# Where the first part's last rows are stored, how many buffers hold a finished block, and how the last two quantised tiles are cut

## The reference, cut to what matters

```python
x = x + xattn(layernorm(x), ctx_512, Wq, Wkv, Wout)   # causal attention, 16 heads
x = x + attn(layernorm(x), w_gate, g_gate, w_down, g_down)
#   bitlinear twice: rmsnorm, rows rounded to 8 bits, weights to -1, 0, 1; 256 -> 2 x 1024 -> 256
x = x + ffn(layernorm(x), gate_w, w_gate, w_up, w_down)
#   16 experts of width 176, each token goes to its best 6, weighted by its softmax scores
return x
```

## Time and profile before

| | |
|---|---|
| three runs, median | 595.3 to 598.86 us, 598.38 us |
| profiled execution | 599.67 us, its span 597.9 us |
| busy, share of the span | PE 83%, DVE 71%, POOL 68%, ACT 59% |
| the barrier between the blocks | about 229 to 230 us |
| the second part's adds (POOL, L1436) | first at 393.6, last at 571.2 us |
| behind the last add | 571.2 to 597.9 us |

### The profile page before, as it was taken

How to read it: one execution, slowest core, us unless ns; L and a number is a source line. 1 busy time by engine, 2 the same in 40 slices (tenths; PEclk the granted TensorE clock), 3 DMA queues, 4 the chain that set the end, 5 groups by cost and what they waited for, 6 DMA issues and landing times.

```text
span 597.9 us, 13765 instructions
## 1 busy us (share of the span) xinstructions
PE 494.3 (83%) x3930; PEld 423.0 (71%) x3952; DVE 427.5 (71%) x1233; ACT 353.2 (59%) x765; POOL 408.5 (68%) x465
## 2 busy tenths in 40 slices
PE   5788999896888865693998999799999999999800
PEld 4567778674555543572998999689998999999800
DVE  5776778868998965797786767367667667668515
ACT  3586665555887973362675666356666666666500
POOL 5743957674886764476777776288887888888860
PEclk9999999979998986596998999799999999999955
DMA  9999994000000004397799775578887888888678
GB/s 253 332 327 328 327 328 159 1 1 2 2 1 2 1 0 147 110 283 244 234 311 301 243 248 192 160 153 149 149 143 132 152 146 146 145 141 138 69 205 320
DMA packets 89653, 100.47 MB, mean 168 GB/s; under 512 B 15328, under 2 KB 83696, under 8 KB 89456
## 3 DMA queue, kind: packets, MB, share of 16 engines
q1 hardware_dynamic: 67744, 69.04, 38.3%
q0 software_dynamic: 18288, 28.72, 25.0%
q10 hardware_dynamic: 3552, 1.84, 1.1%
HBM read 43.11 MB, written 56.46 MB: 167 GB/s over the span
## 4 chain that ended last, share of the span: by engine, by line
PE 32%; DMA 10%; issue 8%; DVE 5%; POOL 3%; ACT 2%; SPq 1%; ACTq 0%; POOLq 0%; DVEq 0%
DMA sums<-x_tok,ids 7%; PE psA L1596 4%; PE psA L1599 4%; PE psA L1597 4%; PE psT L1575 3%; POOL sums L1436 3%; PE psT L1579 3%; PE psY L1612 2%; DMA w_experts<-sums 2%; PE psY L1613 2%; PE psY L1615 2%; PE psY L1614 2%; PE psY L1616 2%; PE psDown L1521 1%; SPq L1368 1%
## 5 line engine op out<-in xcount | busy, mean ns | idle before, releaser
L1436 POOL DMA_INDIRECT sums<-x_tok,ids x87 | 135.1, 1553 | 30.5 <-issue 18.0
L1410 POOL DMA_INDIRECT slots<-h_rows,slot x96 | 93.7, 976 | 43.1 <-issue 40.2
L1931 DVE TENSOR_TENSOR hp_lo<-psT,hp_hi 128x512 fp32r<-128x512 f32 (+1 forms) x132 | 87.9, 667 | 25.0 <-ACT hp_hi L1702 14.8
L1702 ACT ACTIVATE hp_hi<-psT 128x512 fp32r<-128x512 f32 (+1 forms) x132 | 76.4, 579 | 19.6 <-PE psT L1575 9.7
L1596 PE MATMUL psA<-w_experts,hp_lo 128*128 x252 | 84.6, 336 | 2.9 <-DVE hp_lo L1931 1.6
L1918 DVE SCALAR_TENSOR_TENSOR act<-psA,share,sg 128x128 f32<-128x128 f32 x126 | 44.2, 351 | 59.2 <-ACT sg L1709 57.9
L1599 PE MATMUL psA<-w_experts,hp_hi 128*128 x252 | 82.7, 328 | 0.0
L1597 PE MATMUL psA<-w_experts,hp_hi 128*128 x252 | 82.6, 328 | 0.0
L1709 ACT ACTIVATE sg<-psA 128x176 f32<-128x176 f32 x126 | 40.0, 317 | 63.7 <-PE psA L1599 63.4
L1714 ACT ACTIVATE x_tok<-psY 128x256 f32<-128x256 f32 x126 | 48.5, 385 | 30.7 <-DMA sums<-x_tok,ids 21.7
L1612 PE MATMUL psY<-w_experts,hp_lo 128*128 x126 | 46.5, 369 | 7.4 <-DVE hp_lo L1931 4.0
(11 more groups left out here) (266 smaller groups left out, 1396.8 us busy)
## 6 DMA issues: line engine op xcount, KB each, us to landing
x_tok<-slots SPq DMA_DIRECT2D x126, 144.0 KB
slots<-pad_row SPq DMA_DIRECT2D x1, 12528.0 KB, 58.2
slots<-pad_row SPq DMA_DIRECT2D x1, 5616.0 KB, 20.0
w_experts<-sums SPq DMA_DIRECT2D x12, 384.0 KB, 8.2
y_rows<-x_tok SPq DMA_DIRECT2D x29, 128.0 KB, 3.4
sums<-pad_row SPq DMA_DIRECT2D x2, 1664.0 KB, 13.4
d_stage<-in_L_ffn_w_down_dram SPq DMA_DIRECT2D x16, 176.0 KB
wg_nat<-in_L_attn_w_gate_dram SPq DMA_DIRECT2D x1, 2048.0 KB, 16.1
```

What stands on the lines that cost most here:

```text
L1410: pool.indirect_dma_start(out=k.slots[q], out_offset=bass.IndirectOffsetOnAxis(ap=slot[:, n, j:j + 1], axis=0), in_=hrow[:, n, :], in_offs ...
L1436: pool.indirect_dma_start(out=k.sums[i % SUMS], out_offset=bass.IndirectOffsetOnAxis(ap=ids[:, i % IDS:i % IDS + 1], axis=0), in_=y[t % YB ...
L1702: nc.scalar.activation(hp_hi[:, p % 2, first:end, :], psT[p % 2][:, first:end, :], ACT.Copy).then_inc(s_hi, 1)
L1931: nc.vector.tensor_tensor(hp_lo[:, p % 2, first:end, :], psT[p % 2][:, first:end, :], hp_hi[:, p % 2, first:end, :].bitcast(F32), ALU.subt ...
```

## The change

Three things.

1. **Quantised stage.** For tiles 14 and 15 the eight transposes, ACT's copy and the eight matmuls are done in two halves of four; each half has its own semaphore count (`turns`, `halves`).
2. **Second part's blocks.** Eight buffers in place of four: the old ones and four slices of `gu_stage`, the staging area of expert weights, whose last weights are used in the first part. Eight blocks have to pass before a buffer is written again. The PSUM result goes alternately to `psY` and `psDown`, so that PE waits for the copy of two blocks ago. Columns for row numbers: 16 in place of 8. The first part's blocks stay as they were.
3. **The end.** SP stores tile 2 ahead of its wait for the last adds. DVE adds tile 3's gathered rows behind chunk 1 (`LAST_GATHERED`), and SP stores tile 3 ahead of chunk 2.

```diff
+HALVED = NT - 2
+def turns(n):
+    return n + max(n - HALVED, 0)
+def halves(n):
+    return (slice(0, IC),) if n < HALVED else (slice(0, IC // 2), slice(IC // 2, IC))
...
                 def hq_out(n):
-                    need(act, s_hqT, n + 1)
                     need(act, s_down, n - 1)
-                    nc.scalar.activation(hqT[:, n % 2, :, :], psH[:, :, :], ACT.Identity, bias=rounder[:, 1:2]
-                                         ).then_inc(s_hqTsb, 1)
+                    for part, c in enumerate(halves(n)):
+                        act.wait_ge(s_hqT, turns(n) + part + 1)
+                        nc.scalar.activation(hqT[:, n % 2, c, :], psH[:, c, :], ACT.Identity, bias=rounder[:, 1:2]
+                                             ).then_inc(s_hqTsb, 1)
...
                 def h_transposed(n):
...
-                    for c in range(IC):
-                        last = nc.tensor.transpose(psH[:, c, :], hr[:, n % 2, c * P:(c + 1) * P], k.ident[:, :])
-                    last.then_inc(s_hqT, 1)
+                    for part in halves(n):
+                        for c in range(part.start, part.stop):
+                            last = nc.tensor.transpose(psH[:, c, :], hr[:, n % 2, c * P:(c + 1) * P], k.ident[:, :])
+                        last.then_inc(s_hqT, 1)
...
                 def down(n):
-                    need(pe, s_hqTsb, n + 1)
...
+                    for part, cs in enumerate(halves(n)):
+                        pe.wait_ge(s_hqTsb, turns(n) + part + 1)
+                        for c in range(cs.start, cs.stop):
...
-IDS = 8
+IDS = 16
+DEEP = 8
...
+        spare = [k.gu_stage[n // 2][:, n % 2, :] for n in range(DEEP - YBUF)]
+        deep = [y[(NA + n) % YBUF] for n in range(YBUF)] + spare
+        def y_of(t):
+            return y[t % YBUF] if t < NA else deep[(t - NA) % DEEP]
...
-        psOut = psY[:, 0:D]
+        psOut = [psY[:, 0:D], psD[:, 0:D]]
...
+        LAST_GATHERED = 1
...
+                for n in range(len(OUT_AT), LOOP_TILES):
+                    first_part_out(n)
                 for a in range(SUMS):
                     sp.wait_ge(s_acc[a], 16 * NB // SUMS)
...
                 for c in range(CHUNKS):
+                    if c == LAST_GATHERED + 1:
+                        for n in range(LOOP_TILES, TA):
+                            first_part_out(n)
                     sp.wait_ge(s_add, 2 * c + 2)
                     sp.dma_start(k.out_v[:, TA + CHUNK * c:TA + CHUNK * (c + 1), :], fin(c, 0)).then_inc(s_out, 16)
-                for n in range(len(OUT_AT), TA):
-                    sp.wait_ge(s_fa, 4 * n + 4)
-                    sp.dma_start(k.out_v[:, n, :], k.x[:, n, :]).then_inc(s_out, 16)
...
-                    if t >= 1:
+                    out = psOut[t % 2 if t >= NA else 0]
+                    if t > NA:
+                        pe.wait_ge(s_y, t - 1)
+                    elif t >= 1:
                         pe.wait_ge(s_y, t)
...
-                    buffer_free(act, t - YBUF)
-                    nc.scalar.activation(y[t % YBUF], psOut, ACT.Copy).then_inc(s_y, 1)
+                    if t < NA + YBUF:
+                        buffer_free(act, t - YBUF)
+                    elif t >= NA + DEEP:
+                        buffer_free(act, t - DEEP)
+                    nc.scalar.activation(y_of(t), psOut[t % 2 if t >= NA else 0], ACT.Copy).then_inc(s_y, 1)
...
-                    if c >= CHUNKS - TA + LOOP_TILES:
-                        for turn in range(4):
-                            gathered(c - CHUNKS + TA, turn)
+                    if c == LAST_GATHERED:
+                        for n in range(LOOP_TILES, TA):
+                            for turn in range(4):
+                                gathered(n, turn)
```

More of the change, by code:

```diff
@@ L1051, in down @@
                     need(pe, s_x2, n)
-                    for c in range(IC):
-                        last = nc.tensor.matmul(psD, hqT[:, n % 2, c, :], k.wdT[:, c, :], start=(c == 0),
-                                                stop=(c == IC - 1))
+                    for part, cs in enumerate(halves(n)):
+                        pe.wait_ge(s_hqTsb, turns(n) + part + 1)
+                        for c in range(cs.start, cs.stop):
+                            last = nc.tensor.matmul(psD, hqT[:, n % 2, c, :], k.wdT[:, c, :], start=(c == 0),
+                                                    stop=(c == IC - 1))
                     last.then_inc(s_down, 1)
@@ L1340, in block_rows, with first_part_out @@
                     sp.dma_start(hin[t % HIN], k.slots[q][i * P:(i + 1) * P, :]).then_inc(s_hin[t % HIN], 16)
+                def first_part_out(n):
+                    sp.wait_ge(s_fa, 4 * n + 4)
+                    sp.dma_start(k.out_v[:, n, :], k.x[:, n, :]).then_inc(s_out, 16)
                 def next_expert(e):
@@ L1438, in add_rows @@
                         out_offset=bass.IndirectOffsetOnAxis(ap=ids[:, i % IDS:i % IDS + 1], axis=0),
-                        in_=y[t % YBUF], in_offset=None, compute_op=ALU.add).then_inc(s_acc[i % SUMS], 16)
+                        in_=y_of(t), in_offset=None, compute_op=ALU.add).then_inc(s_acc[i % SUMS], 16)
                 for q in range(NPART):
@@ L1608, in back @@
                         pe.wait_ge(s_dlo, t + 1)
-                    if t >= 1:
+                    out = psOut[t % 2 if t >= NA else 0]
+                    if t > NA:
+                        pe.wait_ge(s_y, t - 1)
+                    elif t >= 1:
                         pe.wait_ge(s_y, t)
                     hi, lo = aT_hi[buf], aT_lo[buf]
-                    nc.tensor.matmul(psOut, lo[:, 0, :], weights(off, OFF_D0), start=True, stop=False)
-                    nc.tensor.matmul(psOut, hi[:, 0, :], weights(off, OFF_D0_LO), start=False, stop=False)
-                    nc.tensor.matmul(psOut, hi[:, 0, :], weights(off, OFF_D0), start=False, stop=False)
-                    nc.tensor.matmul(psOut, lo[:, 1, :], weights(off, OFF_D1), start=False, stop=False)
-                    nc.tensor.matmul(psOut, hi[:, 1, :], weights(off, OFF_D1), start=False, stop=True).then_inc(s_G2, 1)
+                    nc.tensor.matmul(out, lo[:, 0, :], weights(off, OFF_D0), start=True, stop=False)
+                    nc.tensor.matmul(out, hi[:, 0, :], weights(off, OFF_D0_LO), start=False, stop=False)
+                    nc.tensor.matmul(out, hi[:, 0, :], weights(off, OFF_D0), start=False, stop=False)
+                    nc.tensor.matmul(out, lo[:, 1, :], weights(off, OFF_D1), start=False, stop=False)
+                    nc.tensor.matmul(out, hi[:, 1, :], weights(off, OFF_D1), start=False, stop=True).then_inc(s_G2, 1)
                 pe.wait_ge(s_table, NPART)
```

8 lines of the change are left out of this document (3 added, 5 removed).

## The result

The changed kernel takes 595.41 us (median of 15 runs, 591.15 to 597.12); the kernel before took 598.38 in 15 runs beside it. The ratio is 0.9942, with a 95% interval of 0.9921 to 0.9963: 3.5 us less by the ratio, between 2.2 and 4.7; the two medians lie 3.0 apart. The forecast was 596.1, 2.3 less, at the edge of that interval. The profiled execution of after took 592.29 us (span 590.6), 7.4 less than the one of before. Half of that isn't the change; the split is further down.

A forecast was written before the change was run, and what follows sets the result against it. The prediction took POOL's queue of adds and gathers to bound the loop; quantised stage -1.0, buffers 0 and end -1.3 sum to -2.3 us, giving 596.1 us on the median's scale, range 592.5 to 599.3.

The forecast's parts named there:

- What bounds the loop: Second part's loop: POOL's queue, 1.85 us per add and 1.39 per gather, sets the pace; ACT's 21.7 us are its echo.
- the rival priced at 586.5: Second part's loop: POOL lacks blocks, so with more buffers it goes at PE's 2.00 us a block; 586.5 us, chance 0.03.
- POOL's 4.7 us: Adds, first to last: 177.7 us against 173.0 without waits; POOL stood still 4.7 us for landings of adds three blocks before.
- 0.76 us later: POOL's adds: the waiting add starts 0.76 us behind the needed landing, so landings up to 4.79 us are hidden.
- The quantised stage: Tiles 14 and 15 in halves: residual, statistics, POOL's power and the barrier come 1.0 us earlier (-0.5 to -1.1).
- The 1.83 that the prediction halved: Tile 14's eight transposes took 1.83 us; four were taken to be done after half of that.
- The end: Behind the last add: DVE without a gap, chunk 3 last, its store landed at 596.2 against 597.5; -1.3 us.
- The loop: Second part with eight buffers and two banks: ACT's waits go, POOL's instructions and landing waits stay; 0 us.
- Copies are done earlier, adds are not: Second part's loop: the step by which eight buffers take ACT's 21.7 us of waits away and gain 0 us.
- the fast rival: Loop: an even pace shortens landings, POOL's 4.7 us of waits go, loop runs at 173.0; 591.4 us, chance 0.14.
- The slow rival: Loop: PE no longer held, block loads crowd the adds, landings lengthen to a mean of 5.4 us; 603.0 us, chance 0.07.
- the prediction's estimate of 3.84 us: An add's landing: 128 KB land 2.3 us after POOL's 1.54, 3.84 in all, so no add would ever wait.

The follow-up runs named there:

- e4: The changed kernel with tile 2's six gathers moved on POOL from between the adds to behind the last add; 594.62 us, ratio 0.9955.
- e1: The kernel before with only the halves of tiles 14 and 15; 597.32 us against 597.49, ratio 0.9983.
- e5: The changed kernel with four arrays of sums in place of three; adds 173.42 us, one execution 598.91 us.
- e7: e4 with four buffers and one PSUM bank again; adds 172.61 us, one execution 599.88 us.
- e3: The kernel before with only the new order at the end; 597.20 us, ratio 0.9977.
- e2: The kernel before with only the eight buffers, two PSUM banks and 16 columns of row numbers; 596.66 us, ratio 0.9971.
- e13: e5 with four buffers and one PSUM bank; adds 173.87 us, one execution 598.37 us.
- e12: The changed kernel, eight buffers kept, but ACT waits for the add four blocks back; adds 175.33 us, one execution 594.74 us.
- e10: The kernel before with second-part block loads cut to half their columns from the eighth block on (wrong output); adds 175.74 us, one execution 597.36 us.
- e11: The changed kernel with second-part block loads cut to half their columns (wrong output); adds 175.50 us, one execution 591.36 us.
- e6: The changed kernel with two tiny POOL writes to dead memory ahead of every add; adds 179.60 us, one execution 600.43 us.

## Why the prediction was right, and where a term was off

- **What bounds the loop.** Right, and shown. ACT's waits vanished (21.7 us to none) and POOL issued its adds almost as before. e4 shows it from the other side: 8.3 us of instructions off POOL's queue, 8.3 us off the adds. The rows that pointed at the buffers were an echo: PE's gaps and ACT's waits moved, the time didn't. By the rule on repeated gaps of the Trainium skill, "Perfetto Trace Analysis", section "Optimization Strategy", the loop would have gone at PE's pace, the rival priced at 586.5. This trace doesn't bear that out: the gaps went and the adds still took 176.16 us, since the gaps were on ACT, which wasn't the full engine.
- **POOL's 4.7 us.** Landings are right for most of it, "stood still" is not right for all: POOL's gaps come to 4.0 us, the rest is adds that took longer to make up than 1.54. And a landing isn't always followed by the next add 0.76 us later. The longest gap of before is this:

```profile
455.39 1.54 POOL L1436 DMA_INDIRECT sums<-x_tok,ids  x1 [2.22 <-DMA sums<-x_tok,ids]
```

  It ended 1.65 us behind the landing of the add that was needed (447.90 + 5.84 = 453.74). What held the other 0.9 us isn't shown.
- **The quantised stage**, forecast -1.0: -0.93 in after's profile, but only -0.43 in e1's. Over all profiles the drain took 8.64 to 9.71 us in the ten kernels with halves (median 9.15) and 10.03 to 10.85 in the four without (median 10.26): 1.1 less, and no kernel of the one kind in the range of the other. The two copies of 128x512 took 1.27 us together, 0.68 each by the mean of their line (they overlap a little), where I took 0.60. The barrier came at 227.33, 9.10 behind the transposes; I had said 229.4 on the scale of before, 9.0 behind them. The scatter within a kind goes with PE's granted clock in the drain, which the prediction didn't ask about. Here are the first 2 us from the transposes' start in e1 and in e5 (columns as in the first row above):

```profile
220.39:222.39 2.00, 1.97 (x8) 1.57 (x8) 1.44 (x3) 0.69 (x1) 1.13 (x4) 0.50 0.00 0
...
221.75:223.75 2.00, 1.51 (x12) 1.17 (x12) 1.43 (x3) 1.25 (x3) 1.13 (x4) 1.00 0.00 0
```

  At 0.50 (1.2 GHz) the eight transposes took 1.97 us and the drain 9.60; at 1.00 (2.4 GHz) 1.09 and 8.64. Ahead of the transposes PE had stood 1.04 us for ACT in both, so why the clock fell in one isn't shown. The 1.83 that the prediction halved was itself read at 0.61. Where the transposes took the same time, 1.83 in before and 1.82 in e7, the halves bring 0.9 us (10.03 against 9.17).
- **The end**, forecast -1.3: -1.29 in after, -1.5 in e3; among the nine profiles with three arrays and the old places of the gathers, 25.03 to 25.43 us in the five with the new order and 26.24 to 26.67 in the four with the old. DVE without a gap, chunk 3 last, as said. The span ended 3.0 us behind the last store's issue; I had 2.5 plus the 0.4 behind the last landing of before, 2.9.
- **The loop**, forecast 0: this is the term that was off, if any was. The adds took 1.5 us less. The step was "Copies are done earlier, adds are not": the adds still wait for landings, but POOL lost 3.2 us in place of 4.7. The direction is that of the fast rival, of which a third came. The slow rival, later landings because PE no longer stops, did not come. Part of the 1.5, or all of it, may be scatter: with four buffers the adds took 176.83, 177.67 and 179.08 in three executions, with eight 176.16 and 176.16. No eight is above any four, but five executions are few, and POOL's gaps were 2.6 us in e1 with four buffers and 2.5 in after with eight; e2's ratio, -0.3% with an interval from -0.6% to 0, says the same in time. How near the total came to the forecast is in part luck: the loop's 1.5 us and the 0.5 us by which the drains of after and e1 differ with the clock are both outside its working.

**What stays open** is whether the adds land sooner with the new buffers at all, and if so why. Shown: POOL's gaps are landings (e5, e13), and it isn't that ACT and PE stop less (e12). Against it stand the landings that the views could match, in e1 with four buffers and below in e2 with eight:

```profile
DMA to landing us min/median/max: 3.7/3.9/5.0
...
DMA to landing us min/median/max: 3.7/4.0/5.7
```

These are no shorter with eight. A single late landing can make the difference: the one gap of 2.22 us in before gives 1.9 of its 4.0. Not separated: the place of the four further buffers, the second bank, the loads' bytes (e10, e11), and scatter between executions.

On the landing itself the Trainium skill, "DMA: Bandwidth & Descriptors", section "Anatomy of one DMA", led to the prediction's estimate of 3.84 us. The median of after, 4.0, is close to it; the later landings, up to 5.4, it doesn't give, and for those POOL pays.

## What to carry to other kernels

Before buffers are added for an engine that waits, ask who empties them: if that engine already issues one instruction after another with only its fixed gap between, more buffers take the visible waits away and win little or no time. Count its queue from the timeline, gaps included, since the busy share leaves them out; then take instructions off that queue first, and the buffers may pay afterwards (e7 against e4: 4.7 us, one profile each). When work is moved from a full queue to the end, look at what the end waits for: e4 gave back there most of what it had won.

## What the runs showed of the hardware that was not expected

- POOL's small writes are almost free beside indirect transfers: two of them per add, 0.61 us each by the trace, cost 0.02 us per add in e6; the rows above show one running while the transfer before it is made up.
- A copy of 128x1024 out of PSUM into bf16 takes 1.11 us, two of 128x512 take 1.27: two copies in place of one cost 0.16 us of ACT, and pay only through the earlier start of what waits.
- The stretch from the barrier to the first add, the same instructions in all fourteen profiles, took from 159.6 to 163.4 us. That scatter of one stage, 3.8 us, is as large as the whole effect of the change, 3.5.
- PE's granted clock over the first 2 us of the drain's transposes was 0.50 to 0.72 in twelve of the fourteen profiles, 0.96 in e3 and 1.00 in e5. With halves, the drain took 8.64 us at 1.00 and 9.60 to 9.71 at 0.50 to 0.53.
